# Value products of four key tiles at a time instead of two, and a new table of where projections and maxima stand

## The chip, the cores and the metric

The kernel runs on one core of a Trainium2 chip. Four compute engines of the core matter here: TensorE (PE in the profile, with PEld for its weight loads), VectorE (DVE), ScalarE (ACT) and GpSimd (POOL). SyncE (SP) issues the transfers. Each engine runs its own list of instructions in order and waits on semaphores for the others. The metric is the device time of one execution in microseconds (us).

## What is computed

A decoder layer: causal self-attention over 56 tokens, cross-attention to 1500 context rows with a relative position bias, and a feed-forward block, each followed by a residual sum and a layer norm. There are 32 batch elements ("batches" below), 16 heads of width 8. The change is in the cross-attention, whose reference is

```
q = shape(query_states @ wq, T)
k = shape(key_value_states @ wk, S)
v = shape(key_value_states @ wv, S)
bias = compute_bias(rel_bias, T, S)
scores = jnp.einsum('bhtd,bhsd->bhts', q, k) + bias
weights = jax.nn.softmax(scores, axis=-1)
attn = jnp.einsum('bhts,bhsd->bhtd', weights, v)
...
return attn @ wo
```

with T = 56, S = 1500, D = 128.

## The kernel before

`cross_attention_block` walks `u` from -2 to 32, one value of `u` for each batch, and inside it `j` from 0 to 11, one step for each tile of 128 keys (`ST` = 12; the last tile has 92). All engines follow the same two loops. What is done in a step:

- **Scores** (`scores`, line 611): two halves of four matmuls, keys on the partitions, 448 columns a half, for batch `u`. They go to `st_ps`, three banks in turn (`ST_BANKS`), so the second half of a step waits for the exponential of three halves ago.
- **Near add** (line 720): in steps 0 and 1 VectorE adds the position bias of the near keys to the two halves.
- **Exponential** (line 799): ScalarE turns each half into `e_sb`, a ring of `E_RING` tiles.
- **Value products** (`value_pair`, lines 641 and 650): `e_sb` times the values `vals`, summed over all tiles in `pv_ps`. TensorE does them in four column groups of 32 at once. Before, they come in pairs of tiles: at every odd step, two tiles that were exponentiated earlier. The profile counts each of these fp32 matmuls twice, so a pair shows as 16 + 8 records.
- **Maxima** (`max_chunk`, line 113): the softmax needs the row maximum before the scores are taken. So the scores of a later batch are computed a second time, queries on the partitions, in 24 chunks of 476 or 512 columns (numbers 0 to 23) into three banks (`MAX_BANKS`), and VectorE reduces each (line 120 for the eight near chunks, line 123 for the others). Chunk 0 stands at step 8 of the walk two batches ahead, chunk 23 at step 7 one batch ahead. Before, each step has two.
- **Negated maximum**: at step `NM` = 7, behind chunk 23, VectorE makes the bf16 parts of the maximum (lines 732 to 741, `nm3`). At step `NMT` = 9 TensorE transposes them (line 669, "nmt"), ScalarE copies the result (line 790) and SyncE puts it into the query stack.
- **One bank `misc`** takes turns in the table `MISC`, whose entries are (kind, part, how many batches ahead): three parts "k" of the key projection (line 687, 500 columns each), three parts "v" of the value projection (line 692, four tiles each), "den", the softmax denominators of the batch before (lines 698 and 699), and nmt. Each waits in `misc_free` until ScalarE has emptied the bank. A "k" part is copied twice (line 820 to bf16 `kpart`, line 781 to `k_left` in the next step) and GpSimd splits the rest (lines 845 to 851). "v" is copied by lines 769 and 771.
- Other work of VectorE at fixed steps: two reciprocals of the denominators at steps 4 and 5 (lines 746 and 748), and the end of the batch at step 7 (lines 724 and 753).

Within a step TensorE's order is: scores, the first maximum, nmt if it stands there, the value products, the other maxima, then the projection or den. For the start (`u` = -2 and -1) a table of its own, `HEAD_MISC`, holds the projections. SyncE first stores the rest of the queries (`store_q`, line 105), waits for it, and only then enters the walk, whose first transfer is `load_ctx` of batch 2 (line 872), needed by the first "k" part.

## Time and profile before

| | value |
|---|---|
| median of 3 runs | 1006.11 us (1005.04 to 1008.34) |
| the profiled execution | 1014.0 us, of which the trace spans 1012.2 us |
| PE, PEld busy | 93%, 64% of the span |
| DVE busy | 72% |
| ACT busy | 60% |
| POOL busy | 37% |

Three stretches make up the span: the self-attention until 90 us, the cross-attention from 90 to 850 us, and the feed-forward block behind it. The shares are means over all three; in the feed-forward block VectorE and ScalarE do little, so in the cross-attention their shares are higher. The rows further down are of that stretch. The time of the profiled execution is 7.9 us above the median of the timed runs.

### The profile page before, as it was taken

How to read it: one execution, taken by the hardware profiler on the slowest of the kernel's cores; microseconds unless marked ns; L12 is line 12 of the kernel's file. 1: busy time of each engine (PE TensorE's matmuls, PEld its weight loads, DVE VectorE, ACT ScalarE, POOL GpSimd, SP SyncE). 2: the span in 40 equal slices, each digit the busy share in tenths (PEclk: the TensorE clock that was granted, in tenths of full speed). 3: DMA queues.
4: the chain of work that ended last, by engine and by line, in shares of the span. 5: the costliest groups of instructions: out<-in, count | busy, mean ns of one | idle time of the engine just before them, and what ended most of it. 6: DMA issues, size and time to landing. Idle time of an engine off the chain costs nothing. (4 is left out here: it accounts for less than half of the span.)

```text
span 1012.2 us, 26082 instructions
## 1 busy us (share of the span) xinstructions
PE 937.9 (93%) x10410; PEld 648.6 (64%) x10410; DVE 727.5 (72%) x1705; ACT 610.4 (60%) x1423; POOL 376.2 (37%) x317
## 2 busy tenths in 40 slices
PE   6776599999999999999999999999999987899996
PEld 3543267777777777777777767777777766455564
DVE  5657488888888888888888888888888853520023
ACT  2322277777777677777777677777777663532232
POOL 7300344445555544445555544445555100000000
PEclk9866799999999999999999999999999998899998
DMA  8736376766656667677666676776665403000001
GB/s 202 248 82 139 108 222 184 205 199 202 188 178 191 193 204 203 199 200 200 190 181 191 193 201 192 203 204 198 195 176 161 131 2 94 25 1 0 1 10 27
DMA packets 56324, 154.96 MB, mean 153 GB/s; under 512 B 23234, under 2 KB 35322, under 8 KB 53114
## 3 DMA queue, kind: packets, MB, share of 16 engines
q1 hardware_dynamic: 55820, 152.44, 52.4%
q8 instruction: 82, 1.34, 0.6%
q10 hardware_dynamic: 384, 0.86, 0.3%
q14 instruction: 38, 0.31, 0.1%
HBM read 110.03 MB, written 42.63 MB: 151 GB/s over the span
## 5 line engine op out<-in xcount | busy, mean ns | idle before, releaser
L799 ACT ACTIVATE e_sb<-st_ps 128x448 f32<-128x448 f32 (+1 forms) x768 | 384.0, 555 | 85.3 <-DVE st_ps L720 59.7
L123 DVE TENSOR_REDUCE cmax<-max_ps 112x1 f32<-112x512 f32 x512 | 334.0, 681 | 90.5 <-PE max_ps L113 87.8
L113 PE MATMUL max_ps<-kst,qst 111*112 111x512 bf16 (+1 forms) x768 | 270.1, 393 | 7.2 <-PEq L132 3.7
L611 PEld LDWEIGHTS st_ps<-qst,kst 114*128 114x128 bf16 (+1 forms) x3072 | 196.5, 101 | 98.5 <-ACT e_sb L799 37.2
L611 PE MATMUL st_ps<-qst,kst 114*128 114x112 bf16 (+1 forms) x3072 | 233.2, 213 | 8.8 <-ACT e_sb L799 3.0
L845 POOL TENSOR_TENSOR kpart<-k_left,kpart 128x500 bf16<-128x500 f32 x90 | 102.0, 1134 | 229.7 <-ACT k_left L781 229.7
L120 DVE CUSTOM_DVE_ANT_0 near_out<-max_ps,near_nat 112x476 bf16<-112x476 f32 x256 | 152.3, 649 | 12.7 <-PE max_ps L113 12.7
L641 PE MATMUL pv_ps<-e_sb,vals 128*32 128x168 f32 (+1 forms) x3072 | 150.1, 313 | 0.0
L851 POOL TENSOR_TENSOR kpart<-k_left,kpart 128x500 bf16<-128x500 f32 x90 | 125.7, 1397 | 7.1
L113 PEld LDWEIGHTS max_ps<-kst,qst 111*112 111x112 bf16 x768 | 86.0, 131 | 51.8 <-issue 27.8
L692 PEld LDWEIGHTS misc<-wv,ctxt 128*128 128x128 f32 (+1 forms) x768 | 97.8, 190 | 17.8 <-ACT vals L771 11.8
L641 PEld LDWEIGHTS pv_ps<-e_sb,vals 128*32 128x32 f32 (+1 forms) x3072 | 80.8, 109 | 40.0 <-issue 20.9
L692 PE MATMUL misc<-wv,ctxt 128*128 128x128 f32 (+1 forms) x768 | 105.4, 280 | 0.9 <-ACT vals L771 0.8
L848 POOL TENSOR_TENSOR k_left<-k_left,kpart 128x500 f32<-128x500 f32 x90 | 102.4, 1138 | 7.1
L687 PE MATMUL misc<-ctxt,wk 128*128 128x500 f32 x180 | 92.3, 594 | 9.6 <-DMA ctxt<-in_ctxT 9.2
L820 ACT CAST kpart<-misc 128x500 bf16<-128x500 f32 x90 | 51.8, 575 | 76.6 <-PE misc L687 76.6
L859 POOL TENSOR_TENSOR x_own<-x_sb,own 128x280 f32<-128x280 f32 x32 | 21.0, 655 | 163.7 <-ACT x_sb L808 163.7
L1131 DVE TENSOR_TENSOR y<-ff_ps,s 112x512 f32<-112x512 f32 x4 | 2.8, 690 | 97.2 <-PE ff_ps L1029 97.2
L650 PE MATMUL pv_ps<-e_sb,vals 128*32 128x112 f32 (+1 forms) x1536 | 72.3, 260 | 0.0
L769 ACT COPY vals<-misc 128x384 f32<-128x384 f32 (+2 forms) x128 | 51.1, 400 | 30.7 <-PE misc L692 30.7
L720 DVE TENSOR_TENSOR st_ps<-st_ps,near_t 18x144 f32<-18x144 f32 (+1 forms) x128 | 53.3, 459 | 4.8 <-PE st_ps L611 4.8
L650 PEld LDWEIGHTS pv_ps<-e_sb,vals 128*32 128x32 f32 (+1 forms) x1536 | 50.3, 110 | 4.7
(126 smaller groups left out, 894.9 us busy)
## 6 DMA issues: line engine op xcount, KB each, us to landing
kst<-kparts SPq DMA_DIRECT2D x192, 375.0 KB, 6.8
kparts<-kpart SPq DMA_DIRECT2D x90, 375.0 KB, 2.7
ctxt<-in_ctxT SPq DMA_DIRECT2D x31, 750.0 KB, 7.8
qst<-qslots SPq DMA_DIRECT2D x192, 28.0 KB, 6.9
qslots<-qst SPq DMA_DIRECT2D x4, 672.0 KB, 12.2
kparts<-kst SPq DMA_DIRECT2D x6, 375.0 KB, 3.3
h<-in_h SPq DMA_DIRECT2D x2, 1024.0 KB, 8.8
qslots<-kst SPq DMA_DIRECT2D x24, 56.0 KB, 3.2
```

The costliest lines, as they stand in the source:

```text
L113: return nc.tensor.matmul(dst[0:TT, 0:hi - lo], m.qst[0:M_ROW, r, p, :], m.kst[0:M_ROW, r, p, lo:hi], start=True, stop=True)
L120: return nc.vector.tensor_tensor_reduce(out=m.near_out[:, p % MAX_BANKS, :], in0=src[0:TT, 0:FIRST_CH], in1=m.near_nat[:, p, :], scale=1.0 ...
L123: return nc.vector.tensor_reduce(m.cmax[:, r, c, p:p + 1], src[0:TT, 0:BOUND[c + 1] - BOUND[c]], AX.X, ALU.max)
L611: mm = nc.tensor.matmul(st_ps[0:K, w % ST_BANKS, p * TT:(p + 1) * TT], m.kst[0:AUG, u % RING, 4 * h + p, j * P:j * P + K], m.qst[0:AUG, u ...
L641: nc.tensor.matmul(pv_ps[32 * q:32 * q + 32, 0:A_COLS], m.vals[0:K, u % 2, j, 32 * q:32 * q + 32], e_sb[0:K, j % E_RING, q * A_COLS:(q + 1 ...
L650: mm = nc.tensor.matmul(pv_ps[32 * q:32 * q + 32, A_COLS:A_COLS + B_COLS], m.vals[0:K, u % 2, j, 32 * (4 + i):32 * (5 + i)], e_sb[0:K, j % ...
L687: nc.tensor.matmul(misc[:, 0:CH], wk[:, :], ctxt[:, r, part * CH:(part + 1) * CH], start=True, stop=True).then_inc(s_kp, 1)
L692: mm = nc.tensor.matmul(misc[0:st_rows(t), i * C:(i + 1) * C], ctxt[:, r, t * P:t * P + st_rows(t)], wv[:, :], start=True, stop=True)
L799: nc.scalar.activation(e_sb[0:K, j % E_RING, h * HALF:(h + 1) * HALF], st_ps[0:K, w % ST_BANKS, 0:HALF], ACT.Exp).then_inc(s_ex, 1)
L845: nc.gpsimd.tensor_tensor(kpart[:, 1, cols], k_left[:, cols], kpart[:, 0, cols], ALU.subtract).then_inc(s_kr, 1)
L848: nc.gpsimd.tensor_tensor(k_left[:, cols], k_left[:, cols], kpart[:, 0, cols], ALU.subtract).then_inc(s_kr, 1)
L851: nc.gpsimd.tensor_tensor(kpart[:, 2, cols], k_left[:, cols], kpart[:, 1, cols], ALU.subtract).then_inc(s_k3, 1)
```

## The change

Value products come four tiles at a time (`VT` = 4), at steps 1, 5 and 9; the ring of exponent tiles grows from four to six. The two tables become one: two "v" parts move to steps 10 and 11 two batches ahead, "k" parts stand at 0, 4 and 7 instead of 4, 5 and 7. Steps 1, 5 and 9 hold no projection. A new table `MANY` gives each step one to three maxima. The ScalarE copies of the "k" part of step 7 both stand behind the first exponential of step 8 (`LATE_K`). At the start the context of batch 2 is loaded ahead of everything else on SyncE's list. The number of matmuls, copies and reductions is the same.

```diff
 A_COLS, B_COLS = 3 * T, 2 * T
 PIECES = 5
-E_RING = 4
+E_RING = 6
+VT = 4
...
-        PAIRED = ST // 2
+        QUADS = ST // VT
         NMT = M0 + 1
-        HEAD_MISC = {1: ("v", 0, 1), 2: ("v", 1, 1), 3: ("v", 2, 1), NMT: ("nmt", 0, 1),
-                     4: ("k", 0, 3), 5: ("k", 1, 3), 7: ("k", 2, 3)}
-        MISC = {0: ("v", 0, 1), 1: ("v", 1, 1), 2: ("v", 2, 1), 3: ("den", 0, -1),
-                4: ("k", 0, 3), 5: ("k", 1, 3), 7: ("k", 2, 3), NMT: ("nmt", 0, 1)}
+        MISC = {10: ("v", 0, 2), 11: ("v", 1, 2), 2: ("v", 2, 1), 3: ("den", 0, -1),
+                0: ("k", 0, 3), 4: ("k", 1, 3), 7: ("k", 2, 3), NMT: ("nmt", 0, 1)}
+        LATE_K = (7,)
+        MANY = {8: 1, 9: 3, 10: 2, 11: 2, 0: 2, 1: 3, 2: 2, 3: 2, 4: 2, 5: 3, 6: 1, 7: 1}
...
         def max_items(g, u, j):
 
-            for i in range(2):
-                lag, n = (1, 2 * (j + ST - M0) + i) if j < M0 else (2, 2 * (j - M0) + i)
+            lag = 1 if j < M0 else 2
+            first = sum(MANY[(M0 + i) % ST] for i in range((j - M0) % ST))
+            for n in range(first, first + MANY[j]):
                 if live(g, u + lag):
                     yield lag, n, n // PAIRS, n % PAIRS
 
         def misc_user(g, u, j):
 
-            user = (HEAD_MISC if u < 0 else MISC).get(j)
+            user = MISC.get(j)
...
-            def value_pair(g, u, t):
+            def value_tiles(g, u, t):
 
                 n = batch(g, u)
-                wait(pe, s_ex, 2 * (n * ST + t + 2))
+                wait(pe, s_ex, 2 * (n * ST + t + VT))
                 if t == 0:
                     wait(pe, s_xr, n)
                     wait(pe, s_ve, 3 * n + 3)
...
-                for j in (t, t + 1):
+                for j in range(t, t + VT):
...
-                    pv = (g, u - 1, ST - 2) if j == 1 else (g, u, j - 3)
-                    if j % 2 and live(g, pv[1]):
-                        value_pair(*pv)
-                    if chunks:
-                        max_chunk(g, u, chunks[1])
+                    pv = (g, u - 1, ST - VT) if j == 1 else (g, u, j - VT - 1)
+                    if j % VT == 1 and live(g, pv[1]):
+                        value_tiles(*pv)
+                    for item in chunks[1:]:
+                        max_chunk(g, u, item)
                     if not user or user[0] == "nmt":
                         continue
                     kind, part, lag = user
-                    if u == -1:
+                    if u < 0:
...
+            def first_of_k(g, u, j):
+
+                kind, part, lag = misc_user(g, u, j)
+                n = batch(g, u + lag)
+                act.wait_ge(s_kp, 3 * (n - SA_K) + part + 1)
+                if n > SA_K:
+                    act.wait_ge(s_k3, 3 * (n - SA_K - 1) + part + 1)
+                if part == 0:
+                    wait(act, s_kw[0], 16 * (n - SA_K))
+                nc.scalar.copy(kpart[:, 0, part * CH:(part + 1) * CH], misc[:, 0:CH])
+
             def rest_of_k(g, u, j):
 
                 user = misc_user(g, u, j)
                 if user and user[0] == "k":
+                    if j in LATE_K:
+                        first_of_k(g, u, j)
                     cols = slice(user[1] * CH, (user[1] + 1) * CH)
                     nc.scalar.copy(k_left[:, cols], misc[:, 0:CH]).then_inc(s_kf, 1)
...
                     if live(g, u):
                         K = st_rows(j)
-                        wait(act, s_pv, b * PAIRED + j // 2 - 1)
+                        if b * ST + j >= E_RING:
+                            act.wait_ge(s_pv, (b * ST + j - E_RING) // VT + 1)
...
-                        if kind == "k":
-                            act.wait_ge(s_kp, 3 * (n - SA_K) + part + 1)
-                            if n > SA_K:
-                                act.wait_ge(s_k3, 3 * (n - SA_K - 1) + part + 1)
-                            if part == 0:
-                                wait(act, s_kw[0], 16 * (n - SA_K))
-                            cols = slice(part * CH, (part + 1) * CH)
-                            nc.scalar.copy(kpart[:, 0, cols], misc[:, 0:CH])
+                        if kind == "k" and j not in LATE_K:
+                            first_of_k(g, u, j)
...
-                if live(g, u + 4):
+                if live(g, u + 4) and u > FIRST:
                     if live(g, u + 1):
                         sp.wait_ge(s_vp, 3 * (b + 2))
                     load_ctx(b + 4, u + 4)
...
+            load_ctx(FIRST + 4, FIRST + 4)
             sp.dma_start(m.wo[:, :, :], d["wo"]).then_inc(m.s_wo, 16)
             sp.dma_start(own[:, :], d["own"]).then_inc(s_own, 16)
```

How this moves instructions. TensorE, before, from the scores of step 7 to the value products of step 9 (`st_ps` scores, `max_ps` maxima, `pv_ps` value products, `misc<-ctxt` the "k" part, `misc<-ident_b,nm` nmt):

```order
257 L611 MATMUL st_ps<-qst,kst 128x112 x8
258 L113 MATMUL max_ps<-kst,qst 112x512
259 L641 MATMUL pv_ps<-e_sb,vals 32x168 x8
260 L650 MATMUL pv_ps<-e_sb,vals 32x112 x4
261 L113 MATMUL max_ps<-kst,qst 112x512
262 L687 MATMUL misc<-ctxt,wk 128x500
263 L611 MATMUL st_ps<-qst,kst 128x112 x8
264 L113 MATMUL max_ps<-kst,qst 112x476 x2
265 L611 MATMUL st_ps<-qst,kst 128x112 x8
266 L113 MATMUL max_ps<-kst,qst 112x476
267 L669 MATMUL misc<-ident_b,nm 24x112
268 L641 MATMUL pv_ps<-e_sb,vals 32x168 x8
```

Value products stand at steps 7 and 9 here, four matmul rows apart. TensorE after the change, from the end of the value products of step 5 to nmt in step 9:

```order
223 L652 MATMUL pv_ps<-e_sb,vals 32x112 x8
224 L114 MATMUL max_ps<-kst,qst 112x512 x2
225 L613 MATMUL st_ps<-qst,kst 128x112 x8
226 L114 MATMUL max_ps<-kst,qst 112x512
227 L613 MATMUL st_ps<-qst,kst 128x112 x8
228 L114 MATMUL max_ps<-kst,qst 112x512
229 L689 MATMUL misc<-ctxt,wk 128x500
230 L613 MATMUL st_ps<-qst,kst 128x112 x8
231 L114 MATMUL max_ps<-kst,qst 112x476
232 L613 MATMUL st_ps<-qst,kst 128x112 x8
233 L114 MATMUL max_ps<-kst,qst 112x476
234 L671 MATMUL misc<-ident_b,nm 24x112
```

The value products that stood in step 7 are gone from between the last maxima and nmt, two maxima (numbers 20 and 21) stand directly behind the value products of step 5, and steps 6, 7 and 8 have one each.

VectorE over the same place, before, from the first reciprocal to the last part of the negated maximum:

```order
135 L746 RECIPROCAL rec<-den 128x168
136 L123 TENSOR_REDUCE cmax<-max_ps 112x1 x2
137 L748 RECIPROCAL rec<-den 128x112
138 L123 TENSOR_REDUCE cmax<-max_ps 112x1 x2
139 L724 TENSOR_TENSOR rec<-x_own,rec 128x280
140 L123 TENSOR_REDUCE cmax<-max_ps 112x1 x2
141 L732 TENSOR_REDUCE pv_ps<-cmax 112x8
```

and after:

```order
135 L748 RECIPROCAL rec<-den 128x168
136 L124 TENSOR_REDUCE cmax<-max_ps 112x1 x3
137 L750 RECIPROCAL rec<-den 128x112
138 L124 TENSOR_REDUCE cmax<-max_ps 112x1
139 L726 TENSOR_TENSOR rec<-x_own,rec 128x280
140 L124 TENSOR_REDUCE cmax<-max_ps 112x1
141 L734 TENSOR_REDUCE pv_ps<-cmax 112x8
```

The work is the same; one reduction moved ahead of the first reciprocal and one ahead of the second.

SyncE at the start, before: the stores of the queries, then the walk with the two context loads of batches 2 and 3.

```order
30 L105 DMA qslots<-kst 64x8x56 x12
31 L913 DMA kst<-kst 15x12000
32 L913 DMA kst<-kst 3x12000
33 L872 DMA ctxt<-in_ctxT 128x1500 x2
34 L875 DMA kparts<-kpart 128x1500
```

and after, where the load of batch 2 stands ahead of what is shown:

```order
30 L918 DMA own<-in_own 128x5
31 L106 DMA qslots<-kst 64x8x56 x12
32 L924 DMA kst<-kst 15x12000
33 L924 DMA kst<-kst 3x12000
34 L882 DMA ctxt<-in_ctxT 128x1500
```

One of the two loads behind the stores is gone from there.

## Rows read from the trace of the kernel before

**Rows 1.** Busy time of each engine in a stretch of steady batches; columns in the header.

```profile
core 0: us, PE busy (x) PEld busy (x) DVE busy (x) ACT busy (x) POOL busy (x), PEclk, DMA share, GB/s
400.00:525.00 125.00, 123.96 (x1642) 89.52 (x1640) 108.14 (x246) 92.57 (x229) 59.96 (x52) 1.00 0.71 201
```

**Rows 2.** Timeline of GpSimd: start, length, instruction, idle before; one row a batch.

```profile
174.87 0.66 POOL L859 TENSOR_TENSOR x_own<-x_sb,own 128x280 f32<-128x280 f32 x1 [3.70 <-ACT x_sb L808]
...
561.71 0.66 POOL L859 TENSOR_TENSOR x_own<-x_sb,own 128x280 f32<-128x280 f32 x1 [3.71 <-ACT x_sb L808]
```

**Rows 3.** Timeline of TensorE's matmuls, steps 5 to 7 of one batch.

```profile
567.93 0.38 PE L113 MATMUL max_ps<-kst,qst 111*112 111x512 bf16 x1
568.24 0.78 PE L641 MATMUL pv_ps<-e_sb,vals 128*32 128x168 f32 x16
568.84 0.38 PE L650 MATMUL pv_ps<-e_sb,vals 128*32 128x112 f32 x8
569.14 0.42 PE L113 MATMUL max_ps<-kst,qst 111*112 111x512 bf16 x1
569.40 1.00 PE L687 MATMUL misc<-ctxt,wk 128*128 128x500 f32 x2
570.24 0.56 PE L611 MATMUL st_ps<-qst,kst 114*128 114x112 bf16 x8
570.64 0.60 PE L113 MATMUL max_ps<-kst,qst 111*112 111x512 bf16 x2
571.07 0.82 PE L611 MATMUL st_ps<-qst,kst 114*128 114x112 bf16 x8
```

**Rows 4.** The same timeline, the transpose of the negated maximum in step 9.

```profile
575.52 0.37 PE L113 MATMUL max_ps<-kst,qst 111*112 111x476 bf16 x1
575.82 0.22 PE L669 MATMUL misc<-ident_b,nm 112*24 112x112 bf16 x1
```

**Rows 5.** The same timeline, two "v" parts with one step between, a batch later.

```profile
583.48 1.06 PE L692 MATMUL misc<-wv,ctxt 128*128 128x128 f32 x8
584.37 0.56 PE L611 MATMUL st_ps<-qst,kst 114*128 114x112 bf16 x8
584.77 0.60 PE L113 MATMUL max_ps<-kst,qst 111*112 111x512 bf16 x2
585.27 1.15 PE L692 MATMUL misc<-wv,ctxt 128*128 128x128 f32 x8
586.26 0.56 PE L611 MATMUL st_ps<-qst,kst 114*128 114x112 bf16 x8
```

**Rows 6.** Timeline of VectorE, second reciprocal to the negated maximum, same batch as rows 3.

```profile
570.21 0.84 DVE L748 RECIPROCAL rec<-den 128x112 f32<-128x112 f32 x1
571.06 1.29 DVE L123 TENSOR_REDUCE cmax<-max_ps 112x1 f32<-112x512 f32 x2
572.26 0.44 DVE L724 TENSOR_TENSOR rec<-x_own,rec 128x280 f32<-128x280 f32 x1
572.62 1.47 DVE L123 TENSOR_REDUCE cmax<-max_ps 112x1 f32<-112x512 f32 x2
...
574.96 0.17 DVE L741 TENSOR_TENSOR nm<-pv_ps,nm 112x8 bf16<-112x8 f32 x1
```

**Rows 7.** Timeline of TensorE at the start of the cross-attention, first "k" part and first scores.

```profile
112.36 2.01 PE L687 MATMUL misc<-ctxt,wk 128*128 128x500 f32 x2 [9.20 <-DMA ctxt<-in_ctxT]
...
124.75 0.56 PE L611 MATMUL st_ps<-qst,kst 114*128 114x112 bf16 x8
```

**Rows 8.** Timeline of SyncE's transfer issues at the same place.

```profile
91.14 8.55 SPq L105 DMA_DIRECT2D qslots<-kst  x12
...
105.42 2.56 SPq L872 DMA_DIRECT2D ctxt<-in_ctxT  x2
```

**Rows 9.** Source view of line 872, its transfers' time to landing.

```profile
DMA to landing us min/median/max: 6.0/7.8/10.7
```

**Rows 10.** View of the transfers from 90 to 105 us: packets and their sizes.

```profile
DMA packets 7170, 0.91 MB, mean 60 GB/s; under 512 B 7040, under 2 KB 7168, under 8 KB 7168
```

More of the change, by code:

```diff
@@ L644, in value_pair @@
                                          start=(j == 0), stop=(j == ST - 1), skip_group_check=True)
-                for j in (t, t + 1):
+                for j in range(t, t + VT):
                     K = st_rows(j)
@@ L805, in iteration @@
                     if j == 1 and live(g, u - 1):
-                        act.wait_ge(s_pv, b * PAIRED)
+                        act.wait_ge(s_pv, b * QUADS)
                         wait(act, s_ro, b - 1)
```

## The prediction

> **What bounds the kernel now.** I read the busy shares first, then the period of a batch, then the timelines of TensorE and VectorE over one batch, and last the start. In the steady stretch TensorE is busy 123.96 of 125 us, VectorE 108.14 (87%), ScalarE 92.57 (74%) [rows 1]. So TensorE sets the pace, VectorE is close behind it. GpSimd's one row a batch gives the period: 17 batches from 174.87 to 561.71, 22.76 us each [rows 2]. "Busy" hides TensorE's small stalls, since the ends of matmuls are modelled, so I go by starts.
>
> Starts of successive groups give these bricks [rows 3]: a step's scores 0.39 us (570.24 to 570.64); a maximum 0.22 (two in 0.43 up to 571.07); from the maximum ahead of a value pair to the pair 0.31 (567.93 to 568.24), so 0.09 more than between maxima; the pair 0.90 (568.24 to 569.14), of which the first 16 records take 0.60 and the last 8 take 0.30; the first maximum behind it 0.26; a "k" part 0.84 (569.40 to 570.24). A "v" part takes 0.89 [rows 5], den about 0.5 by the same reckoning. From a maximum to nmt is 0.30 [rows 4]; the value products follow at once. The 0.09 and the end of a pair are costs of switching between whole-array matmuls and column groups.
>
> **The change, term by term, per batch.**
>
> *Quads.* Six pairs become three quads. Two pairs cost 1.80. A quad is the same 48 records without the inner switch. Four rounds of 0.14 us make up the 0.60, and the last 8 records stream in about 0.19 of their 0.30, so a quad is 2 x 0.60 + 0.19 + 0.30 = 1.66 after rounding; at worst it stays 1.80. Each merge also saves one entry (0.09) and one slow first maximum (0.04). Sum: 3 x (0.14 + 0.09 + 0.04) = 0.8 us saved, with a floor of 0.4 if a quad is 1.80. The Trainium skill, "TensorEngine Tiling (Array Packing)", Key Properties, says that changing the tiling mode drains TensorE; by that the saving stands as computed, and the rows on the switch agree with it (0.09 us going in).
>
> *The negated maximum.* This is the term that decides. nmt needs chunk 23 reduced and five small VectorE instructions behind it. Before, VectorE is done at 575.13 [rows 6], TensorE arrives at 575.82 [rows 4]: 0.69 us of slack. After, let m be the start of chunk 20, the first maximum behind the quad of step 5. VectorE is then idle (chunk 19 stands 1.97 us earlier) and has ahead of it: chunk 20's end and hand-over 0.46 (it runs 0.42 [rows 3]), reductions 20 and 21 at 0.60 each, the second reciprocal 0.80 (it lasts 0.84 and overlaps its successor a little), reduction 22 at 0.60, line 724 at 0.36 (572.26 to 572.62), reduction 23 at 0.69 and the chain of the negated maximum 1.04 (its predecessor ends at 572.62 + 1.47 = 574.09, it ends at 575.13) [rows 6]. Sum 5.15, and 0.05 for the semaphore: m + 5.2. TensorE, from m: chunks 20 and 21 0.48, scores 0.39, chunk 22 0.22, scores of step 7 with the wait for an exponential 0.65 (the row of 0.82 instead of 0.56 in a step that follows a short one [rows 3]), chunk 23 0.22, "k" 0.84, scores 0.39, chunk 0 0.21, scores with the same wait 0.66, chunk 1 to nmt 0.30. Sum 4.36. TensorE waits 0.84 us, and the quad of step 9, two maxima and everything later stand behind nmt. The value products that stood in step 7 were the cover. Bounds: 0.5 if every VectorE term is 5% shorter and TensorE meets its small waits earlier, 1.0 if the wait for the exponential in step 9 vanishes.
>
> *The late copy of the "k" part.* Both copies come behind the first exponential of step 8, so the bank is free about 2.0 us after the part's end; nmt is wanted 1.56 after it (0.39 + 0.21 + 0.66 + 0.30). Alone it would cost 0.4, but it ends before the negated maximum does (m + 2.80 + 2.0 = m + 4.8), so it costs nothing beside it. If the VectorE term were absent, 0.4 would be left.
>
> *Projections side by side.* "v" at 11 directly follows "v" at 10, "k" at 0 follows "v" at 11, den at 3 follows "v" at 2, each with only scores and two maxima between, while ScalarE copies the bank. That pattern exists before: the second of two "v" parts starts 0.50 behind the maxima instead of 0.43 and takes 0.99 instead of 0.89 [rows 5], together 0.17. Before it occurs once a batch, and den had a pair ahead of it. After: 0.17 + 0.17, and den 0.28 since the third "v" part is copied in four pieces; less the one of before, 0.17. Net 0.45. Low end 0.2, if the "k" part and den lose only the 0.07.
>
> *Maxima behind a quad.* The last chunks of steps 2 and 10 come 1.07 us behind the first chunk after the quad, whose bank they need; it is reduced 0.46 + 0.69 later. About 0.13 each, 0.26; low end 0.
>
> *Waits that go.* The scores of step 1 waited for the near add, 0.18, and those of step 11 for an exponential, 0.1. Both get longer work ahead of them: 0.28 gained. The ring of six adds no wait: a tile is needed again only after the quad that TensorE has done by then.
>
> Sum per batch: -0.8 + 0.84 + 0.45 + 0.26 - 0.28 = +0.47, from -0.2 (all low ends) to +0.9. For the 28 batches in which all kinds of work are present that is +13 us, from -6 to +25.
>
> **The start.** TensorE waits 9.20 us for the context of batch 2 and begins its "k" part at 112.36; the first scores are at 124.75 [rows 7]. The load is issued at 105.42, behind the query stores issued from 91.14 and a wait for their landing [rows 8]. After, it is issued at about 90.3 and lands 7.8 us later (6.0 to 10.7) [rows 9], at 96 to 101. In these 15 us the engines move 60 GB/s [rows 10], so there is room for 750 KB. The "k" part now stands at step 0, ahead of 22 of the 32 maxima of the start. It cannot come before its two "v" parts and ten maxima at the clock of half speed that the 2.01 us of the first "k" part (1.00 in rows 3) show; I put it at 99. Behind it VectorE paces: 14 reductions at 0.60, the negated maximum 1.1, eight near chunks at 0.6, together 14.3, with 3 us of stalls behind "k" and "v" parts and at half clock: first scores near 116.3, 8.5 us earlier than 124.75. Bounds: 5 and 11. The Trainium skill, "DMA: Bandwidth & Descriptors", Specifications, asks for at least 512 B a transfer for line rate, and says that below it the engine does read-modify-write; of 7170 packets in this stretch 7040 are under 512 B [rows 10]. By that rule the load would share the rings with slow stores and land late. Estimated with a landing at twice the median, 106, the "k" part starts 7 us later than I put it and the start gains 1.5 us instead of 8.5.
>
> **The end.** The last quad stands alone behind the last exponential, 0.75 us more than a pair, and the last batch, which ScalarE paces, loses some 0.5 to 1 at its quads; the batch before, with few projections, gains about as much. I take +0.5, from -1 to +2.
>
> **Sum** against the profiled execution's span of 1012.2: 1012.2 + 13 - 8.5 + 0.5 = 1017.2, or +5 us. The profiled execution took 1014.0 in all, 7.9 more than the median 1006.11; the difference of 5 does not depend on that offset. Rounding down a little for terms of mine that may overlap (a wait of one kind swallows part of the next), +4.5: 1010.6 us.
>
> **Rivals.**
> - *Faster, VectorE is not late.* If the reductions are met earlier, nmt is ready when TensorE arrives, and only the 0.4 of the copy or nothing is left. Per batch -0.8 + 0.2 + 0.45 + 0.26 - 0.28 = -0.2, or 28 x -0.2 = -5.6; with the start -13.6: 992.5 us. For it: VectorE has 13% to spare on average [rows 1]. Against it: the chain from m holds no idle time to squeeze. It decides at a wait below 0.3 us.
> - *Level.* The wait at nmt is 0.6 instead of 0.84, all else as above: +0.23 a batch, so 28 x 0.23 - 8.5 + 0.5 = -1.6: 1004.5. It needs VectorE to run 5% faster than its rows, or TensorE to meet 0.24 us more of small stalls ahead of nmt.
> - *Slower still, the start gives nothing,* because the load lands with the stores (above): 1006.11 + 13 - 1.5 + 0.5 = 1018. It decides at a landing past 104.
> - *It doesn't do what it says*: the quad costs 1.80. Then 0.4 a batch more, 1021; nothing in the rows makes the two inner switches survive, as both tiles of a pair already run without one.
>
> **Chances.** Forecast (1006.5 to 1016) 0.50; level 0.2; faster rival 0.15; no gain at the start 0.1; dear quad 0.05. The measurement tells about 0.3% (3 us) from no change. Faster by more than that: the faster rival and a third of level, 0.21. Within: the rest of level and a tenth of the forecast's own spread, 0.2. Slower: 0.59. The range 998 to 1018 leaves out the lower half of the faster rival, the dear quad and part of the last case: 2 in 10.
>
> **What would show it.** Period of a batch 23.2 us (by GpSimd's row) instead of 22.76; a wait of TensorE at nmt for VectorE's line of the negated maximum, some 0.8 us in nearly every batch; a quad of 1.66 us from its first record to the next maximum; the "v" part of step 11 at 0.99; the first scores near 116 and no wait of 9 us for the context. A period under 22.8 with no wait at nmt would make the forecast wrong, first in the term of the negated maximum.

## The result

| | median of the runs | range | against before |
|---|---|---|---|
| before | 1006.43 us (4 runs) | 1005.04 to 1008.34 | |
| after | 1014.15 us (4 runs) | 1012.61 to 1015.31 | 1.008, 95% interval 1.006 to 1.0099 |

The kernel became slower by 7.7 us (6.0 to 10.0 by the interval); the prediction said 4.5, which is in its range but below that interval. The profiled execution of the changed kernel took 1014.47 us, of which the trace spans 1012.7.

**The steady batches.** Busy shares of 400 to 525 us, as in [rows 1], and GpSimd's row of one batch, as in [rows 2] (start, length, instruction, idle before it), both of the changed kernel:

```profile
400.00:525.00 125.00, 120.13 (x1609) 86.25 (x1606) 105.78 (x242) 92.15 (x222) 59.95 (x55) 1.00 0.65 189
```

```profile
188.73 0.66 POOL L869 TENSOR_TENSOR x_own<-x_sb,own 128x280 f32<-128x280 f32 x1 [7.51 <-ACT x_sb L824]
...
560.99 0.66 POOL L869 TENSOR_TENSOR x_own<-x_sb,own 128x280 f32<-128x280 f32 x1 [7.51 <-ACT x_sb L824]
```

TensorE is busy for 120.13 us where it was busy for 123.96. Sixteen batches lie between the two rows, 23.27 us each against 22.76: +0.51 a batch. TensorE from step 5 to the "k" part of step 0, the place of [rows 3 to 5]:

```profile
566.38 0.38 PE L114 MATMUL max_ps<-kst,qst 111*112 111x512 bf16 x1
566.69 1.35 PE L643 MATMUL pv_ps<-e_sb,vals 128*32 128x168 f32 x32
567.85 0.57 PE L652 MATMUL pv_ps<-e_sb,vals 128*32 128x112 f32 x16
568.35 0.64 PE L114 MATMUL max_ps<-kst,qst 111*112 111x512 bf16 x2
568.82 0.56 PE L613 MATMUL st_ps<-qst,kst 114*128 114x112 bf16 x8
...
572.41 0.37 PE L114 MATMUL max_ps<-kst,qst 111*112 111x476 bf16 x1
573.54 0.21 PE L671 MATMUL misc<-ident_b,nm 112*24 112x112 bf16 x1 [0.76 <-DVE nm L743]
573.55 1.34 PE L643 MATMUL pv_ps<-e_sb,vals 128*32 128x168 f32 x32
...
577.90 0.57 PE L114 MATMUL max_ps<-kst,qst 111*112 111x476 bf16 x2
578.40 1.16 PE L694 MATMUL misc<-wv,ctxt 128*128 128x128 f32 x8
579.40 0.56 PE L613 MATMUL st_ps<-qst,kst 114*128 114x112 bf16 x8
579.79 0.60 PE L114 MATMUL max_ps<-kst,qst 111*112 111x512 bf16 x2
580.29 1.11 PE L689 MATMUL misc<-ctxt,wk 128*128 128x500 f32 x2
581.24 0.56 PE L613 MATMUL st_ps<-qst,kst 114*128 114x112 bf16 x8
```

The quad takes 566.69 to 568.35, 1.66 us. From there (m = 568.35) to nmt it is 5.19 us, and the bracket says that TensorE (whose groups of matmuls are shown by their starts) stood idle for 0.76 us of it, released by VectorE's line 743. VectorE in the same batch, the place of [rows 6]:

```profile
568.81 1.29 DVE L124 TENSOR_REDUCE cmax<-max_ps 112x1 f32<-112x512 f32 x2 [0.74 <-PE max_ps L114]
570.01 0.84 DVE L750 RECIPROCAL rec<-den 128x112 f32<-128x112 f32 x1
570.77 0.63 DVE L124 TENSOR_REDUCE cmax<-max_ps 112x1 f32<-112x512 f32 x1
571.32 0.43 DVE L726 TENSOR_TENSOR rec<-x_own,rec 128x280 f32<-128x280 f32 x1
571.67 0.69 DVE L124 TENSOR_REDUCE cmax<-max_ps 112x1 f32<-112x512 f32 x1
572.39 0.19 DVE L734 TENSOR_REDUCE pv_ps<-cmax 112x8 f32<-112x24 f32 x1
...
573.23 0.17 DVE L743 TENSOR_TENSOR nm<-pv_ps,nm 112x8 bf16<-112x8 f32 x1
```

VectorE works through without a gap after the first maximum and ends at 573.40, m + 5.05. The view of waits (engine and line, what it waited for, us in all, times, longest) shows that this happens in nearly every batch, 31 times in all:

```profile
PE misc L671 <- DVE nm L743: 25.2, 31, 1.5
```

**The start.** First maximum, "k" part and first scores, then SyncE's issues, the places of [rows 7] and [rows 8]:

```profile
95.50 1.08 PE L689 MATMUL misc<-ctxt,wk 128*128 128x500 f32 x2 [0.35 <-issue]
...
114.19 0.93 PE L613 MATMUL st_ps<-qst,kst 114*128 114x112 bf16 x8 [2.83 <-DMA qst<-nmp]
```

```profile
87.76 0.35 SPq L882 DMA_DIRECT2D ctxt<-in_ctxT  x1
89.10 9.50 SPq L106 DMA_DIRECT2D qslots<-kst  x12
...
107.83 0.78 SPq L908 DMA_DIRECT2D qst<-nmp  x1
```

The context is in place when the "k" part comes; the wait of 9.20 us is gone. The part itself also takes 1.08 us instead of 2.01: the granted clock is 1.00 (2.4 GHz) from 95.5 to 96.6 us here, and was 0.50 (1.2 GHz) from 112.36 to 114.3 us in the kernel before, behind 9.1 us in which TensorE had done nothing. A wait of 2.83 us for the small transfer of the negated maximum's rows (line 908), which ends some 6.3 us after its issue, stands before the first scores. From the first maximum of the cross-attention to the first scores it was 34.26 us (90.49 to 124.75) and is 26.22 (87.97 to 114.19).

The two spans, 1012.2 and 1012.7, hardly differ, since the profiled execution of the kernel before was 7.6 us above its median. 2.5 us of that is the stage ahead of the cross-attention: its first maximum is at 90.49 there and between 84.8 and 89.4 in the thirteen other traces. So I compare stretches, not spans. From GpSimd's first row of this kind to its last (31 batches) it was 694.04 us, 0.9 of them in one odd batch of 23.63, and is 706.51: +13.4 with that excess taken off. From the first maximum to the first such row it was 61.62 and is 54.24: -7.4. The sum, about +6, lies at the lower edge of the measured 6.0 to 10.0; the traces don't place the rest up to 7.7.

### The profile page after: what moved, and what is told of

The parts are those of the page before. It is cut to its first block and busy times, and to the rows that moved or that the text cites. A ratio compares the mean times of both kernels' runs of the same rounds, so it can differ in the third digit from the quotient of the medians.

```text
span 1012.7 us, 26081 instructions
## 1 busy us (share of the span) xinstructions
PE 927.0 (92%) x10410; PEld 643.2 (64%) x10410; DVE 722.7 (71%) x1705; ACT 617.9 (61%) x1423; POOL 354.6 (35%) x317
## 5 line engine op out<-in xcount | busy, mean ns | idle before, releaser
L124 DVE TENSOR_REDUCE cmax<-max_ps 112x1 f32<-112x512 f32 x512 | 327.0, 677 | 67.3 <-PE max_ps L114 67.1
L114 PE MATMUL max_ps<-kst,qst 111*112 111x512 bf16 (+1 forms) x768 | 258.0, 388 | 4.3 <-PEq L133 2.8
L613 PEld LDWEIGHTS st_ps<-qst,kst 114*128 114x128 bf16 (+1 forms) x3072 | 191.2, 100 | 102.2 <-issue 36.5
L613 PE MATMUL st_ps<-qst,kst 114*128 114x112 bf16 (+1 forms) x3072 | 228.1, 213 | 12.4 <-ACT e_sb L815 3.5
L855 POOL TENSOR_TENSOR kpart<-k_left,kpart 128x500 bf16<-128x500 f32 x90 | 102.6, 1140 | 149.6 <-ACT k_left L796 149.6
L643 PE MATMUL pv_ps<-e_sb,vals 128*32 128x168 f32 (+1 forms) x3072 | 129.3, 309 | 0.9 <-ACT e_sb L815 0.9
L114 PEld LDWEIGHTS max_ps<-kst,qst 111*112 111x112 bf16 x768 | 82.9, 130 | 43.1 <-issue 15.3
L861 POOL TENSOR_TENSOR kpart<-k_left,kpart 128x500 bf16<-128x500 f32 x90 | 102.3, 1137 | 7.1
L643 PEld LDWEIGHTS pv_ps<-e_sb,vals 128*32 128x32 f32 (+1 forms) x3072 | 89.1, 109 | 23.4 <-issue 12.7
L652 PE MATMUL pv_ps<-e_sb,vals 128*32 128x112 f32 (+1 forms) x1536 | 54.4, 259 | 0.0
L796 ACT COPY k_left<-misc 128x500 f32<-128x500 f32 x90 | 52.4, 582 | 0.0
```

The source lines that it names most:

```text
L114: return nc.tensor.matmul(dst[0:TT, 0:hi - lo], m.qst[0:M_ROW, r, p, :], m.kst[0:M_ROW, r, p, lo:hi], start=True, stop=True)
L124: return nc.vector.tensor_reduce(m.cmax[:, r, c, p:p + 1], src[0:TT, 0:BOUND[c + 1] - BOUND[c]], AX.X, ALU.max)
L613: mm = nc.tensor.matmul(st_ps[0:K, w % ST_BANKS, p * TT:(p + 1) * TT], m.kst[0:AUG, u % RING, 4 * h + p, j * P:j * P + K], m.qst[0:AUG, u ...
L643: nc.tensor.matmul(pv_ps[32 * q:32 * q + 32, 0:A_COLS], m.vals[0:K, u % 2, j, 32 * q:32 * q + 32], e_sb[0:K, j % E_RING, q * A_COLS:(q + 1 ...
L855: nc.gpsimd.tensor_tensor(kpart[:, 1, cols], k_left[:, cols], kpart[:, 0, cols], ALU.subtract).then_inc(s_kr, 1)
L861: nc.gpsimd.tensor_tensor(kpart[:, 2, cols], k_left[:, cols], kpart[:, 1, cols], ALU.subtract).then_inc(s_k3, 1)
```

## The experiments

Each was timed beside the kernel before, whose medians there were 1005.4, 1006.71 and 1005.7 us. The recorded ratio is not the quotient of the two medians and differs from it by up to 0.2%, so where two rows are close I go by the periods. The period is that of GpSimd's row over 17 to 19 batches of each trace.

| kernel | median us | ratio to before (95%) | period us |
|---|---|---|---|
| before | | | 22.76 |
| after | 1014.15 | 1.008 (1.006 to 1.0099) | 23.27 |
| e3_before_early_load | 998.98 | 0.9926 (0.9902 to 0.9951) | 22.76 |
| e2_late_load | 1023.84 | 1.0181 (1.0138 to 1.0225) | 23.26 |
| e4_quads_alone | 1019.55 | 1.0141 (1.0097 to 1.0186) | 23.13 |
| e5_no_late_k | 1012.15 | 1.008 (1.0049 to 1.0112) | 23.27 |
| e1_recip_late | 1013.28 | 1.0077 (1.005 to 1.0104) | 23.38 |
| e10_output_later | 1000.86 | 0.9959 (0.9938 to 0.9979) | 22.90 |
| e7_v_apart | 1009.95 | 1.0025 (1.0006 to 1.0045) | 23.19 |
| e12_two_each | 1008.45 | 1.0027 (1.0003 to 1.0052) | 23.12 |
| e13_one_maximum | 1007.80 | 1.0026 (1.0008 to 1.0044) | 23.14 |
| e14_old_projections | 1016.05 | 1.0119 (1.0094 to 1.0144) | 23.10 |
| e8_maxima | 964.31 | 0.9581 (0.9557 to 0.9604) | 21.69 |
| e11_best | 958.07 | 0.952 (0.9494 to 0.9546) | 21.46 |

### The load at the start

The changed kernel with the load of batch 2 back in the walk:

```diff
-                if live(g, u + 4) and u > FIRST:
+                if live(g, u + 4):
...
-            load_ctx(FIRST + 4, FIRST + 4)
```

> The changed kernel with the context load of batch 2 back behind the query stores, where it stands before the change. Theory A (the early load is worth 8 to 9 us at the start): the first k part, now at step 0, waits for a landing near 22 us into the cross-attention instead of starting at 7.5; from it to the first scores it is 16 us without the 2.8 us wait for the small transfer, so first scores at 37.7 instead of 26.2 us: 11.5 us slower, about 1025.5 us, period unchanged at 23.27. Rival B (the gain at the start is taken back by later waits on transfers or by the state of the clock): 1014 to 1018 us.

And the kernel before with those two lines the other way round, and nothing else:

> The kernel before with nothing but the context load of batch 2 moved to the head of SyncE's list. Theory A: the 9.2 us for which TensorE waited before the first k part of step 4 vanish; the rest of the start stands: 997 us, period unchanged at 22.76. Rival B (another transfer, the small one of the negated maximum or the stack of batch 2, lands last then): a gain of 5 us or less, 1001 us or more.

The early load takes 9.7 us off the changed kernel (1023.84 to 1014.15) and 6.4 off the kernel before (5 to 10 by the interval of its ratio), where 9.2 were expected: the median of 998.98 stands between the two theories, nearer to A's 997. In the trace of e3 the stretch from the first maximum to the first scores falls by all of that and more, from 34.26 to 24.12 us; its "k" part takes 1.08 us, at a granted clock of 1.00, where the one behind the wait took 2.01 at 0.50. The periods don't move. In e2 the wait is longer than in [rows 7], because the "k" part now stands ahead of 22 maxima of the start:

```profile
PE misc L689 <- DMA ctxt<-in_ctxT: 12.9, 1, 12.9
```

So the load is worth more in the new order than in the old one, but the new order needs it. Alone on the old kernel it is a gain. The rest of the change costs 15 us beside it (998.98 to 1014.15); the two traces have 13.4 of that over 31 batches and 2.6 over the first one.

### Quads without the rest

The changed kernel with the tables of the kernel before: two maxima in each step, its projections, its copies, its load.

```diff
-        MISC = {10: ("v", 0, 2), 11: ("v", 1, 2), 2: ("v", 2, 1), 3: ("den", 0, -1),
-                0: ("k", 0, 3), 4: ("k", 1, 3), 7: ("k", 2, 3), NMT: ("nmt", 0, 1)}
-        LATE_K = (7,)
-        MANY = {8: 1, 9: 3, 10: 2, 11: 2, 0: 2, 1: 3, 2: 2, 3: 2, 4: 2, 5: 3, 6: 1, 7: 1}
+        MISC = {0: ("v", 0, 1), 1: ("v", 1, 1), 2: ("v", 2, 1), 3: ("den", 0, -1),
+                4: ("k", 0, 3), 5: ("k", 1, 3), 7: ("k", 2, 3), NMT: ("nmt", 0, 1)}
+        LATE_K = ()
+        MANY = {j: 2 for j in range(ST)}
```

> The kernel before with four tiles at a time at steps 1, 5 and 9 and the ring of six alone: its own tables of projections, two maxima a step, no late copy, late load. Theory A (the quad itself saves 0.8 us a batch in drains, but without new tables the waits around it eat more: in steps 0 and 1 for the near add and for the maxima, den right behind the third v part, nmt in step 9, which has no value products of step 7 as cover): period 23.1 to 23.3, start as before, 1016 to 1021 us. Rival B (quads are a clear gain and the new tables are what costs): period 22.0, about 985 us.

It lands in the forecast, with 0.37 us a batch more than the kernel before. A quad saves its 0.14 and its entry here too; waits take more than that back. In the view of waits of e4 (against 11.6 us for the near maxima's bank in the kernel before):

```profile
PEld max_ps L114 <- DVE cmax L121: 23.3, 72, 0.7
PE misc L673 <- DVE nm L745: 9.1, 30, 1.6
```

### The wait at the negated maximum

First, does the late copy of "k" take part in it?

```diff
-        LATE_K = (7,)
+        LATE_K = ()
```

> The changed kernel with one edit: the first copy of "k" is made in its own step 7 again, as in the kernel before, and not in step 8 behind the exponentials. Theory A (at the negated maximum TensorE waits for VectorE, whose rows come 5.05 us after the quad's last record, and ScalarE's late copy is done before that, at 4.74): nothing changes, 1012 to 1016 us, the wait before the transposition stays at 0.76 us with VectorE as its cause. Rival B (the late copy takes part in that wait): the batch falls by 0.2 to 0.4 us, 1003 to 1009 us.

The period stays at 23.27 and the time within the interval of the changed kernel. The bracket at nmt shrinks to 0.54, because the scores of step 9 now wait 0.32 us for an exponential ahead of it; nmt still stands 5.18 us behind m (564.40 to 569.58). The copy costs nothing beside VectorE.

Then VectorE's chain was shortened in three ways. The reciprocals and the output's sums go to steps 8, 9 and 11:

```diff
-        NM, REC_A, REC_B, XH = M0 - 1, 4, 5, 7
+        NM, REC_A, REC_B, XH = M0 - 1, 8, 9, 11
```

> The changed kernel with VectorE's two reciprocals moved from steps 4 and 5 to 8 and 9 and the end of the batch (line 726, line 755) from step 7 to 11. TensorE's and ScalarE's order stays. Theory A (VectorE's chain between the first maximum behind the quad of step 5 and nmt is what TensorE waits for in step 9): the chain loses the second reciprocal (0.76 us) and line 726 (0.35), so the negated maximum is ready 1.1 us earlier. The bank that nmt writes is free only when ScalarE has ended its copy k_left at 573.09 in the trace of the changed kernel, 0.45 before nmt started (573.54), so just 0.35 to 0.4 us of the wait can go: period 23.27 to 22.9, 29 batches, about 1004 us. Rival B (TensorE is held by the projections that stand side by side and by the maxima behind a quad, and the wait at nmt only stands in for waits that would come later): period stays 23.2 to 23.3, 1013 to 1015 us.

The time fell to the rival's side, but the trace shows the first half of theory A: VectorE is done at m + 3.98, and nmt follows at m + 4.80 instead of 5.19, now behind the late copy:

```profile
571.02 0.22 PE L671 MATMUL misc<-ident_b,nm 112*24 112x112 bf16 x1 [0.37 <-ACT k_left L796]
```

The 0.39 us was given back later in the batch, and 0.11 more. The moved work stands among the near maxima of steps 8 to 11, and VectorE comes to the near addition of step 0 1.21 us behind the scores it adds to (576.88 on TensorE), where it was 0.39 (579.40 and 579.79) in the changed kernel; for that addition the exponentials wait, and for them the scores of step 1:

```profile
578.09 1.15 DVE L722 TENSOR_TENSOR st_ps<-st_ps,near_t 128x448 f32<-128x448 f32 x2
```

```profile
579.39 0.37 PE L613 MATMUL st_ps<-qst,kst 114*128 114x112 bf16 x4 [0.30 <-ACT e_sb L815]
```

So the run didn't tell the theories apart: it moved VectorE's lateness. The cleaner edit moves only the output's product and sums, into the step where VectorE had waited 0.69 us:

```diff
-        NM, REC_A, REC_B, XH = M0 - 1, 4, 5, 7
+        NM, REC_A, REC_B, XH = M0 - 1, 4, 5, 8
```

> The changed kernel, with the product and the sums of the finished output's reciprocals moved from step 7 of a batch to step 8, so that VectorE's 0.43 us multiplication no longer stands between the last two maxima of step 7 and the negated maximum; no maximum, quad or projection moves. Theory A (TensorE waits for the negated maximum, and only for it, at this place): the negated maximum is ready some 0.35 us sooner, the wait before its transposition falls from 0.76 to about 0.4 (or goes over to ScalarE's late copy of "k", done 4.75 us after the quad's last record), the batch falls by 0.3 to 0.4 us: 1003 to 1006 us. Unlike the reciprocals of an earlier run, the work that is moved lands in the step after, where VectorE waited 0.69 us for a maximum, so nothing should give it back. Rival B (the batch is set by side-by-side projections and quads, and the wait only absorbs slack): the wait shrinks, others grow, 1012 to 1015 us.

1000.86 us, 13 us less than after and below the forecast 1003 to 1006; 0.36 us a batch less, the forecast size, which makes 10 or 11 of the 13 us. The transposition is at m + 4.82, behind the late copy:

```profile
565.14 0.21 PE L671 MATMUL misc<-ident_b,nm 112*24 112x112 bf16 x1 [0.39 <-ACT k_left L796]
```

The third edit takes one maximum out of step 5:

```diff
-        MANY = {8: 1, 9: 3, 10: 2, 11: 2, 0: 2, 1: 3, 2: 2, 3: 2, 4: 2, 5: 3, 6: 1, 7: 1}
+        MANY = {8: 2, 9: 3, 10: 2, 11: 2, 0: 2, 1: 3, 2: 2, 3: 2, 4: 2, 5: 2, 6: 1, 7: 1}
```

> The changed kernel with one maximum of each batch moved: step 5, which holds a quad, takes two instead of three, and step 8 two instead of one. Nothing else moves but the numbers of the maxima between them. Theory A (VectorE is late at the negated maximum because of what it still has to reduce from the quad of step 5 on: five maxima instead of six is 0.6 us less): the wait before the transposition falls from 0.76 to 0.2 to 0.45 us, the batch by 0.4 to 0.6 us, 998 to 1004 us. Rival B (the batch is set elsewhere): over 1010 us.

Here I was wrong (also in the count: steps 5 to 7 go from five maxima to four, not from six to five): 1007.8 us and a wait of 0.72, 0.13 us a batch gained instead of 0.4 to 0.6. VectorE and GpSimd of e13 at this place:

```profile
564.90 0.63 DVE L124 TENSOR_REDUCE cmax<-max_ps 112x1 f32<-112x512 f32 x1
565.44 0.90 DVE L726 TENSOR_TENSOR rec<-x_own,rec 128x280 f32<-128x280 f32 x1
566.27 0.68 DVE L124 TENSOR_REDUCE cmax<-max_ps 112x1 f32<-112x512 f32 x1
```

```profile
564.90 1.14 POOL L861 TENSOR_TENSOR kpart<-k_left,kpart 128x500 bf16<-128x500 f32 x1
```

VectorE's multiplication takes 0.90 us here and 0.43 in the changed kernel, where it began (571.32) just when GpSimd's instruction had ended (570.18 + 1.13). In e13 it begins 0.54 us later than GpSimd's and ends 0.30 behind it. The view of one tile shows that it is so in most batches (length ns min/median/max over 32):

```profile
L726 DVE TENSOR_TENSOR rec<-x_own,rec x32: 432/896/958, 149.0 to 844.2; 128x280 f32<-128x280 f32 x32
```

The missing 0.47 us is this stretch: taken off, the wait is 0.25, in the forecast range. That is worked out from the rows; no run moved GpSimd's instruction out of the way. The Trainium skill, "SBUF — State Buffer", Who interferes with whom, says that a VectorE instruction with two SBUF inputs contends with a GpSimd instruction that reads SBUF; the rows agree with it, 0.90 us beside such an instruction and 0.43 without.

### Projections side by side

```diff
-        MISC = {10: ("v", 0, 2), 11: ("v", 1, 2), 2: ("v", 2, 1), 3: ("den", 0, -1),
+        MISC = {6: ("v", 0, 2), 11: ("v", 1, 2), 2: ("v", 2, 1), 3: ("den", 0, -1),
```

> The changed kernel with the first part of "v" moved from step 10 to step 6, so that no two parts of a projection of "v" stand in neighbouring steps; the rest is as in the changed kernel. The prediction put a price of 0.17 us a batch on the second part of "v" beside the first one (its "den" and "k" neighbours stay). Theory A (that price is right): the batch falls by 0.1 to 0.2 us, unless the part gives the time back in step 6, ahead of the negated maximum; 1008 to 1014 us. Rival B (neighbouring projections cost nothing): 1013 to 1016 us, with the wait at the negated maximum as it was. Rival C (a projection of 1.0 us before the maxima of step 6 delays the negated maximum): over 1018 us, with a longer wait there.

The batch falls by 0.08 us and the time by 4.2, within theory A's time, below its 0.1 for the batch. The "v" part of step 11 is back at 0.89 (575.82 to 576.71), so the price of the neighbour is real. The moved part, though, stands against the "k" part of step 7, which takes 0.95 instead of 0.84 (568.64 to 569.59); and near maxima without a "v" part between them wait for VectorE (24.1 us in all instead of 14.8). nmt waits for the late copy here.

### The table of maxima and the places of the projections

Two maxima in every step, against the changed kernel's table:

```diff
-        MANY = {8: 1, 9: 3, 10: 2, 11: 2, 0: 2, 1: 3, 2: 2, 3: 2, 4: 2, 5: 3, 6: 1, 7: 1}
+        MANY = {j: 2 for j in range(ST)}
```

> The changed kernel with two maxima in every step, as the kernel before has them; the quads, the moved projections and the late copy stay. Against the changed kernel it undoes the table alone. Theory A (the changed kernel's table does the quads little or no good: it brings the maxima around the quads into a worse order than two each): the batch at 23.0 to 23.2 us, 1006 to 1012 us; the wait at the negated maximum falls to about 0.6 us and one of 0.7 to 0.9 us for a bank of the maxima stands in step 7. Rival B (the table is what makes quads bearable, as its numbers look meant for it): over 1018 us.

The changed kernel's table costs 0.15 us a batch against none at all. VectorE is late in either: two places wait for it instead of one.

```profile
565.15 0.42 PE L114 MATMUL max_ps<-kst,qst 111*112 111x512 bf16 x1 [0.61 <-DVE cmax L124]
...
568.42 0.21 PE L671 MATMUL misc<-ident_b,nm 112*24 112x112 bf16 x1 [0.54 <-DVE nm L743]
```

Both waits are a little below their forecasts (0.6, and 0.7 to 0.9). Now another table. Steps 1 and 5 have one maximum each, which goes ahead of the quad, so that none stands directly behind it; three stand in step 9, where the negated maximum is over, and in 11, 2 and 3, which hold a "v" part or den:

```diff
-        MANY = {8: 1, 9: 3, 10: 2, 11: 2, 0: 2, 1: 3, 2: 2, 3: 2, 4: 2, 5: 3, 6: 1, 7: 1}
+        MANY = {8: 2, 9: 3, 10: 1, 11: 3, 0: 2, 1: 1, 2: 3, 3: 3, 4: 2, 5: 1, 6: 2, 7: 1}
```

> The changed kernel with another table of the maxima alone: steps 8 to 11 and 0 to 7 take 2, 3, 1, 3, 2, 1, 3, 3, 2, 1, 2, 1 of them (before: 1, 3, 2, 2, 2, 3, 2, 2, 2, 3, 1, 1). The steps that hold a quad (1, 5, 9) have one, one and three maxima, the one ahead of the negated maximum three in all instead of six from step 5 on. Quads, projections and the late copy stay. Theory A (the waits of TensorE for VectorE around the quads cost the batch more than the quads save, and they come from the counts in steps 5 and 1): the wait at the negated maximum is gone or set by ScalarE's copy of "k", and the waits for a free bank of the maxima shrink; the batch falls from 23.27 to 21.6 to 22.2 us, the kernel to 966 to 984 us. Rival B (the work side by side and the quads' own time set the batch, at 22.9 or more): 1003 us or more. Rival C (VectorE is the engine that sets the batch, whatever the order): 1010 to 1018 us.

964.31 us, just below the forecast range, with the batch inside it: one line of numbers takes 50 us off the changed kernel, 1.58 a batch. (The expectation's count is off: behind the quad of step 5 it is three maxima instead of four, as in e13. VectorE's multiplication takes 0.44 us here, so it is not stretched.) Cut at its quads, a batch shows where. The three kernels of this table have equal counts of maxima in each stretch (6, 9 and 9); only their places within it differ.

| TensorE, us | quad of step 5 to nmt | nmt to quad of step 1 | to quad of step 5 |
|---|---|---|---|
| after | 6.85 (566.69 to 573.54) | 8.41 (to 581.95) | 8.01 |
| e13_one_maximum | 6.72 (561.41 to 568.13) | 8.41 (to 576.54) | 8.02 |
| e8_maxima | 6.00 (575.24 to 581.24) | 8.07 | 7.60 (567.64 to 575.24) |

The first stretch gains 0.85, half of it at the negated maximum: the wait of 0.83 there is now 0.44, for the late copy. The other half TensorE gains on its own way to it. Behind the single maximum of steps 6 and 8 its next scores waited for an exponential; behind two maxima they hardly do. The scores of steps 7 and 9 took 0.65 and 0.66 us (569.44 to 570.09, 571.75 to 572.41) and take 0.44 and 0.46 (577.74 to 578.18, 580.04 to 580.50); with two maxima in every step (e12) it is 0.43 and 0.46.

```profile
581.24 0.22 PE L671 MATMUL misc<-ident_b,nm 112*24 112x112 bf16 x1 [0.37 <-ACT k_left L796]
```

The other two stretches gain 0.75 between them, out of the prediction's terms "side by side" and "maxima behind a quad". TensorE of e8 in steps 1 to 3:

```profile
567.64 1.35 PE L643 MATMUL pv_ps<-e_sb,vals 128*32 128x168 f32 x32
568.81 0.57 PE L652 MATMUL pv_ps<-e_sb,vals 128*32 128x112 f32 x16
569.31 0.57 PE L613 MATMUL st_ps<-qst,kst 114*128 114x112 bf16 x8
569.72 0.81 PE L114 MATMUL max_ps<-kst,qst 111*112 111x512 bf16 x3
570.37 1.05 PE L694 MATMUL misc<-wv,ctxt 128*128 128x128 f32 x8
571.25 0.56 PE L613 MATMUL st_ps<-qst,kst 114*128 114x112 bf16 x8
571.65 0.85 PE L114 MATMUL max_ps<-kst,qst 111*112 111x512 bf16 x3
572.34 0.48 PE L700 MATMUL misc<-x_sb,sel 128*128 128x168 f32 x2
```

Scores follow the quad at once; three maxima to the "v" part take 0.65, so no bank is waited for; three to den take 0.69, where two took 0.62 in the changed kernel.

Then the projections of the kernel before under this table (the edit of e4_quads_alone with this table in its last line):

> Quads and six buffers, with the projections, the late load and the copies where the kernel before has them, and the table of maxima of the fast kernel: 2, 3, 1, 3, 2, 1, 3, 3, 2, 1, 2, 1 for steps 8 to 11 and 0 to 7. Against the run of quads alone (1019.6 us) it changes the table; against the fast run (964.3 us) it changes the projections' places. Theory A (the table works only with a projection of "v" in steps 10 and 11 and of "k" in step 0, which give VectorE and ScalarE time behind the quads; in steps 0 and 1 they stand on top of the near additions): batch 22.8 to 23.0, 1008 to 1016 us. Rival B (the table alone brings the gain, wherever the projections stand): the batch near 21.7, 970 to 982 us with the late load.

Four kernels with quads form a square, by their periods:

| | two maxima each | the table of e8 |
|---|---|---|
| projections of before | 23.13 (e4) | 23.10 (e14) |
| projections of after | 23.12 (e12) | 21.69 (e8) |

With quads, neither the projections' places nor the table is worth anything alone; together they give 1.4 us a batch. The lower row also has the late copy and the early load, which by e5 and e2 don't move the period. e14 missed its forecast period (22.8 to 23.0) by 0.1, and its 1016.05 us is at the edge of the range. It has almost no wait at nmt left (2.2 us in all), but the most for the bank of the near maxima:

```profile
PEld max_ps L114 <- DVE cmax L121: 31.3, 74, 0.7
```

Without projections in steps 10, 11 and 0, TensorE issues maxima at 0.22 us each there and VectorE reduces them at 0.6; the "v" parts of 0.89 and the "k" part of 0.95 give VectorE time to catch up, if the maxima stand beside them. The trace of e8 has 3.0 us in that line; the difference is 0.9 us a batch. That this is the mechanism is read from the rows, and what makes up the other 0.5 of the 1.4 wasn't traced.

### The best version

The table of e8, no late copy, and the output's sums in step 8:

```diff
-        LATE_K = (7,)
-        MANY = {8: 1, 9: 3, 10: 2, 11: 2, 0: 2, 1: 3, 2: 2, 3: 2, 4: 2, 5: 3, 6: 1, 7: 1}
-        NM, REC_A, REC_B, XH = M0 - 1, 4, 5, 7
+        LATE_K = ()
+        MANY = {8: 2, 9: 3, 10: 1, 11: 3, 0: 2, 1: 1, 2: 3, 3: 3, 4: 2, 5: 1, 6: 2, 7: 1}
+        NM, REC_A, REC_B, XH = M0 - 1, 4, 5, 8
```

> The changed kernel with three edits together: the table of maxima 2, 3, 1, 3, 2, 1, 3, 3, 2, 1, 2, 1 (steps 8 to 11, 0 to 7), the late copy of "k" undone (it is copied in its own step, as the kernel before has it), and the output's product and sums in step 8 instead of 7. Theory A (VectorE's lateness and, behind it, ScalarE's late copy are what TensorE waits for at the negated maximum): both are taken away, the wait there is near zero and the batch 21.3 to 21.8 us, the kernel 958 to 972 us, below the table alone. Rival B (the table alone takes all that is to be had): as the table alone within 0.3%. Rival C (VectorE sets the batch): 1004 us or more.

958.07 us, 4.8% under the kernel before and 6.2 us under the table alone; the two edits beside the table weren't tried apart under it. Busy shares of its steady stretch, and the place of the negated maximum:

```profile
400.00:525.00 125.00, 124.25 (x1766) 94.58 (x1766) 113.55 (x271) 98.07 (x237) 62.47 (x58) 1.00 0.70 207
```

```profile
576.99 0.37 PE L114 MATMUL max_ps<-kst,qst 111*112 111x476 bf16 x1
577.29 0.22 PE L671 MATMUL misc<-ident_b,nm 112*24 112x112 bf16 x1
577.30 1.35 PE L643 MATMUL pv_ps<-e_sb,vals 128*32 128x168 f32 x32
```

The transposition follows the maximum at 0.30 us, with no bracket. VectorE is at 113.55 of 125 us (91%), and TensorE hardly waits. How much of the 1.3 us a batch against the kernel before is the quads' and how much the new order's stays open; pairs in the new order weren't tried.

## Why the prediction was right

Its forecast, slower by 4.5, came out at 7.7, per batch for the reasons it gave, and at the start in part by luck. Step by step:

- **Quads, -0.8.** 1.66 us from the first record to the next maximum, 0.31 ahead of it (566.38 to 566.69), as forecast. (The terms as written, 2 x 0.60 + 0.19 + 0.30, add up to 1.69; the rounding was worth 0.09 a batch, and the trace bears out the 1.66.) The two maxima behind it took 0.47 (568.35 to 568.82), where I had 0.48. Right.
- **The negated maximum, +0.84.** m + 5.19 where the sum was m + 5.2. TensorE's arrival, the last maximum at 572.41 and 0.30 on, is 572.71, m + 4.36 as computed; the wait is 0.83. e10 shows that it is paid: 0.36 us shorter until the late copy is reached, and 0.36 a batch gained.
- **Late copy, 0, but 0.4 if VectorE weren't late.** e5: no change. In e1, e8 and e10 nmt waits for line 796, with 0.37 to 0.39 in the bracket. Both halves right.
- **Side by side, +0.45.** "v" of step 11: 0.50 and 1.00 instead of 0.43 and 0.89 (0.18); "k" of step 0: 0.50 and 0.95 instead of 0.43 and 0.84 (0.18); den starts 0.62 behind the maxima (563.10 to 563.72) and takes 0.59, where it took 0.50 and had no wait ahead of it (0.28). Sizes right. One thing the prediction did not say: in e8 and e11, with three maxima between the two "v" parts, the second takes 0.89. The price is a wait for ScalarE's copy, and one maximum more covers it.
- **Maxima behind a quad, +0.26.** In step 10 the projection stands 0.57 behind the two maxima instead of 0.43 (576.04 to 576.61), in step 2 0.60 (561.22 to 561.82). 0.31 against 0.26.
- **Waits that go, -0.28.** Scores to maximum is 0.40 in step 11 (577.50 to 577.90) and 0.39 in step 1 (581.24 to 581.63), where it was 0.49 and 0.58 in the kernel before: right.
- **Sum +0.47 a batch:** 0.51. This is where the slower time comes from.
- **The start, -8.5.** First maximum to first scores: -8.0; over the first batch -7.4. The "k" part came at 95.50, 7.5 us behind the first maximum instead of the 8.5 I had counted, but the first scores waited 2.83 us for a transfer that I had left out: the negated maximum's rows are issued at 107.83, behind the query stores and four wide transfers. Without that wait it is 15.9 us from the "k" part to the first scores, where I had 17.3: I had counted on half clock, and the granted clock was 1.00 from 93.6 to 111.3 us. The terms that I had too long make 2.4 us, the wait that I left out makes 2.8, and they nearly cancel. That the start came out within about 1 us is in part luck.
- **The load beside small stores.** The rival by the packet rule (a landing at 106) is refuted: the load was issued at 87.76, and "k" began at 95.50 behind its "v" parts with 0.35 of idle time that the trace doesn't put down to it. It stood ahead of the twelve stores issued from 89.10; how a wide load behind such stores fares isn't shown here.
- **The end, +0.5.** The last exponential ends 14.7 us behind the last batch's first one, before 13.8: +0.9 in its range.
- **Total.** +0.04 a batch too little, some 0.5 to 1 at the start too much: +6 from the stretches of the two traces. The rest up to 7.7 is not placed. The step "rounding down a little for overlaps" was the wrong way: the terms per batch did not overlap (0.51 measured, 0.47 added up), and it took the 4.5 below the measured interval.

What the prediction didn't see is how far from its best the order was. It priced each stall as the change had it and never asked where the maxima ought to stand; its two costs of +0.84 and +0.26 both came from where the maxima stood, and so did the waits of 0.65 and 0.66 for an exponential, which it took as given. The 1.6 us that the table of e8 takes off are made of just these terms: 0.4 at the negated maximum, 0.4 of waits for an exponential, 0.75 behind quads and beside neighbours. Moving a few maxima without regard to the rest (e12, e13) gets only 0.15 and 0.13 of it.

## To carry over

When two engines are as close in pace as here (108 and 124 of 125 us busy), count for each step what the leading engine hands over and what other work of its own covers the follower; hand over most where that other work stands, least where the follower has extras or a result is awaited. Behind a long block of the leader, send first what the other engines start from. Test the table of counts and the places of the covering work together: here each alone moved nothing, and the pair moved 1.4 us a batch. A wait that has been removed may return one step later (e1) or uncover the next one (e10, e8), so after each edit read the whole batch and not only the place.

## What the runs showed of the hardware that I had not expected

- VectorE's multiplication of two SBUF tiles took 0.43 us alone and 0.90 while GpSimd added two others (e13); in the kernel before it is GpSimd's instruction that is long in such an overlap:

```profile
571.73 1.97 POOL L851 TENSOR_TENSOR kpart<-k_left,kpart 128x500 bf16<-128x500 f32 x1
```

  It takes 1.14 otherwise, so it is 0.83 longer, beside a multiplication of 0.44 us; what fills the rest isn't shown. In e8 it takes 1.64. So moving either can shift a chain by 0.5 us.
- The transfer of the negated maximum's 24 rows held TensorE up by 0.8 to 2.8 us at the start in the changed kernel and its eight variants with the early load. With the early load alone (e3) it didn't.
- After 9.1 us without a matmul the granted clock was 0.50, and a "k" part took 2.01 us instead of 1.08 (the kernel before against e3). The early load removed that too.
- Periods of a batch repeat to 0.01 us between the traces of kernels with the same order on TensorE (23.27, 23.26 and 23.27; 22.76 twice), while the stage ahead of the cross-attention ends anywhere from 84.8 to 90.5 us. So I read differences per batch to a hundredth, and take a difference of two spans to be uncertain by some 3 us or more.
